# A hybrid layer's second pass reordered: chain slots spread, token rows turned ahead of the second layer's down product

## The reference

```python
x = x + linear_attention(layernorm(x))   # 16 heads, elu(.)+1 feature map, one k^T v matrix per batch, normaliser per head
x = x + ffn(layernorm(x))                # square(relu(x Ws1)) Ws2; routed experts count only where a probability truncates to 1
x = x + small_attention(layernorm(x))    # only the first 16 tokens of each batch, up to 3 softmax iterations; elsewhere a bias row ob
x = x + ffn(layernorm(x))                # the same weights again
```

## Time and profile before

| what | value |
|---|---|
| median of 3 runs (439.25, 441.06, 438.79) | 439.25 us |
| the profiled execution: its time | 441.03 us |
| its span, first to last instruction | 439.2 us |
| PE busy | 404.7 us (92%) |
| DVE busy | 313.5 us (71%) |
| POOL busy | 217.2 us (49%) |
| ACT busy | 204.5 us (47%) |
| mean granted TensorE clock | 0.986 of full speed |

### The profile page before, as it was taken

The page is one execution under the profiler, slowest core; times in us unless marked ns, Lnnn a source line. Parts: engine busy times, 40 slices in busy tenths (PEclk is TensorE's granted clock), DMA queues, the critical chain, the costliest instruction groups (busy, mean ns, idle before and its releaser), DMA issues.

```text
span 439.2 us, 7483 instructions
## 1 busy us (share of the span) xinstructions
PE 404.7 (92%) x2458; PEld 322.7 (73%) x2458; DVE 313.5 (71%) x654; ACT 204.5 (47%) x354; POOL 217.2 (49%) x315
## 2 busy tenths in 40 slices
PE   8898999999999998989989989999899999969983
PEld 5787889988988896777866767677666676747752
DVE  6779976576668666474667688797768877977644
ACT  3766686778778775033324422222342144223340
POOL 3675775776677664032144514662441744533630
PEclk9999999999999999899999999999999999989998
DMA  8701211111100000400011101101110110110022
GB/s 269 236 16 35 80 65 48 49 48 48 48 0 0 1 1 1 99 3 0 6 54 51 52 5 50 52 1 50 49 51 0 51 53 1 50 49 29 22 91 64
DMA packets 22982, 20.64 MB, mean 47 GB/s; under 512 B 3398, under 2 KB 22924, under 8 KB 22924
## 3 DMA queue, kind: packets, MB, share of 16 engines
q1 hardware_dynamic: 22364, 19.40, 14.1%
q10 hardware_dynamic: 560, 0.52, 0.4%
HBM read 11.33 MB, written 8.45 MB: 45 GB/s over the span
## 4 chain that ended last, share of the span: by engine, by line
PE 57%; DVE 18%; ACT 8%; issue 8%; POOL 7%; DVEq 1%; POOLq 0%; ACTq 0%
PE PB L1522 12%; PE PA L1539 11%; PE PT L1557 6%; PE PT L1586 4%; PE PB L1407 3%; ACT scratch L567 3%; PE PG L1358 3%; POOL ln_rstd L444 2%; DVE x_all L1059 2%; ACT scratch L614 2%; POOL ln_rstd L442 2%; DVE ln_bn L797 2%; DVE scratch L1095 2%; ACT xn_pair L578 2%; PE PT L1398 2%
## 5 line engine op out<-in xcount | busy, mean ns | idle before, releaser
L494 POOL TENSOR_TENSOR ln_a<-ln_bn 128x4 f32<-128x4 f32 x32 | 6.7, 210 | 124.2 <-DVE ln_bn L1038 124.2
L1522 PE MATMUL PB<-ws,scratch 128*128 128x256 f32 x248 | 62.3, 395 | 1.9 <-issue 1.9
L1522 PEld LDWEIGHTS PB<-ws,scratch 128*128 128x128 f32 x248 | 46.1, 195 | 20.1 <-issue 14.8
L1539 PE MATMUL PA<-kvwo,q_all 128*128 128x256 f32 x256 | 57.9, 379 | 0.0
L751 ACT ACTIVATE scratch<-PT 128x512 f32<-128x512 f32 x16 | 9.6, 598 | 102.2 <-PE PT L1557 102.2
L1539 PEld LDWEIGHTS PA<-kvwo,q_all 128*128 128x128 f32 x256 | 48.5, 190 | 6.5
L466 POOL TENSOR_TENSOR xn_pair<-scratch,xn_pair 128x1024 fp32r<-128x1024 f32 x16 | 38.5, 2406 | 20.3 <-ACT xn_pair L578 20.3
L882 DVE SCALAR_TENSOR_TENSOR scratch<-scratch,PB 128x512 f32<-128x512 f32 x32 | 20.9, 684 | 38.6 <-ACT scratch L614 38.6
L1038 DVE BATCH_NORM_STATS2 ln_bn<-x_all 128x6 f32<-128x256 f32 x128 | 44.1, 406 | 0.1
L567 ACT ACTIVATE scratch<-x_all,ln_shift,ln_rstd 128x255 f32 (+1 forms) x60 | 31.1, 593 | 22.6 <-POOL ln_shift L448 22.5
L455 POOL TENSOR_TENSOR x_all<-x_all,wvo 128x1024 f32 (+1 forms) x16 | 38.6, 2410 | 0.1
(11 more groups left out here) (252 smaller groups left out, 943.0 us busy)
## 6 DMA issues: line engine op xcount, KB each, us to landing
x_all<-n_L_attn_a_inputs_q_dram SPq DMA_DIRECT2D x15, 512.0 KB, 3.6
out_dram<-x_all SPq DMA_DIRECT2D x15, 512.0 KB, 3.2
out_dram<-x_all SPq DMA_DIRECT2D x2, 256.0 KB, 2.2
x_all<-n_L_attn_a_inputs_q_dram SPq DMA_DIRECT2D x2, 128.0 KB, 3.0
x_all<-n_L_attn_a_inputs_q_dram ACTq DMA_DIRECT2D x2, 128.0 KB, 3.4
setup<-in_L_attn_a_Wk_dram SPq DMA_DIRECT2D x1, 256.0 KB, 4.9
setup<-in_L_attn_a_Wq_dram ACTq DMA_DIRECT2D x1, 256.0 KB, 5.1
wvo<-in_L_attn_a_Wv_dram SPq DMA_DIRECT2D x1, 256.0 KB, 6.4
```

The source lines that it names most:

```text
L1522: last = mm(four(pair)[:, t, :], h[:, t * P:(t + 1) * P], ws2[:, :], start=True, stop=True)
L1539: last = mm(four(PA)[:, t, :], q_all[:, n * C + c, t * P:(t + 1) * P], kvwo[:, b * C + c, :], start=(c == 0), stop=(c == C - 1))
```

## The change

What it does, by engine:

- PE: in a step, R2 stands ahead of F1 (it was behind F4), T2 ahead of F4 (it was behind R2), chain slot 1 ahead of R2, chain slot 2 from step 2 on behind F4, chain slot 3 behind F2. In the last group of the first pass, NP of group 0 stands ahead of the k product (it was behind it).
- DVE: the two inversions are two instructions; that for r opens the step, that for v follows `q_scale`. Chain slot 1 stands ahead of the statistics, h2s ahead of `scaled_sum`, chain slot 3 behind `n_split`. `n_take` and `n_split` of group 0 stand ahead of the last group's k work.
- ACT: it makes the rounded copy n_hi (`n_high`), which DVE made; `scale_tiles` stands behind the copies of T2, chain slot 1 ahead of the relu.
- POOL: the add of the scaled half (now L542) is done a step later, at the step's start, and waits for NP; SP stores a group a step later.

```diff
 # SP
+                u, nu, _ = lagged(g, b, 3)
+                if runs(u):
+                    sp.wait_ge(out_dve, 2 * (u + 1))
+                    sp.wait_ge(out_pool, u + 1)
+                    sp.dma_start(out_dram[bass.ds(nu, 1)].rearrange("o p t d -> p (o t) d"), x_group(nu)).then_inc(stored, 16)
                 if v == NG - 1:
...
-                elif runs(v):
...
-            sp.wait_ge(stored, 16 * (NG - 1))
+            sp.wait_ge(stored, 16 * (NG - 2))
...
 # POOL step
+                if runs(r):
+                    pool.wait_ge(n_mm, min(i + 2, NG))
+                if runs(u):
+                    pool.wait_ge(f4_scaled, 2 * (u + 1))
+                    last = x_all[:, nu * T + 2:(nu + 1) * T, :]
+                    nc.gpsimd.tensor_tensor(last, last, y3, ALU.add).then_inc(out_pool, 1)
                 if runs(r):
...
                     add_row(nr, ob_rows, ob_added)
-                ge(pool, rsq, i - 1)
                 if runs(v):
+                    ge(pool, rsq3, v)
                     four_variances(1, v, bn3, var3)
                 chain(i, 1)
...
-                if runs(v) and v < NG - 1:
-                    pool.wait_ge(f4_scaled, 2 * (v + 1))
-                    last = x_all[:, nv * T + 2:(nv + 1) * T, :]
-                    nc.gpsimd.tensor_tensor(last, last, y3, ALU.add).then_inc(out_pool, 1)
...
 # ACT
+            def n_high(j):
+
+                act.wait_ge(n_inv, j + 1)
+                ge(act, n_op_done, j)
+                nc.scalar.activation(n_hi[:, :], n_sb[:, :], ACT.Copy).then_inc(n_hi_done, 1)
...
                 if i == 0:
+                    n_high(1)
                     fold_ffn()
+                chain(i, 1)
                 if runs(r):
...
-                if runs(v) and v < NG - 1:
-                    scale_tiles(i, v)
-                chain(i, 1)
                 if runs(i):
...
+                if runs(v) and v < NG - 1:
+                    scale_tiles(i, v)
...
                 chain(i, 2)
+                if runs(i + 2):
+                    n_high(i + 2)
...
 # DVE
-                dve.wait_ge(n_inv, 2 * j + 1)
-                nc.vector.tensor_copy(n_hi[:, :], n_sb[:, :]).then_inc(n_inv, 1)
...
+            def reciprocal_variances(slot, j, ready, used, done):
+
+                dve.wait_ge(ready, 5 * (j + 1))
+                ge(dve, used, j if slot == 0 else 2 * j)
+                nc.vector.reciprocal(ln_rsq[:, slot, :], ln_a[:, slot, :]).then_inc(done, 1)
...
+                if runs(r):
+                    reciprocal_variances(0, r, var2, r2_mm, rsq)
                 if runs(i):
...
-                if i > 0:
-                    reciprocal_variances(i, r, v)
+                if runs(v):
+                    reciprocal_variances(1, v, var3, f4_scaled, rsq3)
+                chain(i, 1)
                 if runs(i):
...
-                if runs(v):
-                    scaled_sum(i, v, nv)
-                chain(i, 1)
                 if runs(r):
...
                     nc.vector.tensor_tensor(h2s, h2, PT[:, 1, :], ALU.mult).then_inc(f1_scaled, 1)
+                if runs(v):
+                    scaled_sum(i, v, nv)
                 chain(i, 2)
                 if runs(i + 2):
                     n_take(i + 2)
-                chain(i, 3)
...
                 if runs(i + 2):
                     n_split(i + 2)
+                chain(i, 3)
...
 # PE, first pass
                 ge(pe, k_done, 2 * n)
+                if isinstance(n, int) and n == NG - 1:
+                    n_product(0, 0, 0)
...
                     k_product(n, g, b)
-                    if last and g == G - 1:
-                        n_product(0, 0, 0)
 # PE, step
+                chain(i, 1)
+                if runs(r):
+                    pe.wait_ge(rsq, r + 1)
...
+                    for t in range(T):
+                        last = nc.tensor.transpose(PT[:, 1, t * P:(t + 1) * P], ln_rsq[:, 0, t:t + 1].to_broadcast([P, P]), ident[:, :])
+                    last.then_inc(r2_mm, 1)
                 if runs(r):
...
                     last.then_inc(f1_mm, 1)
+                if runs(i):
+                    pe.wait_ge(w_added, i + 1)
+                    for c in range(C):
+                        for t in range(T):
+                            last = nc.tensor.transpose(PA[:, c, t * P:(t + 1) * P], x_all[:, n * T + t, c * P:(c + 1) * P], ident[:, :])
+                        last.then_inc(t2_mm, 1)
                 if runs(v):
...
                     down(PB if v < NG - 1 else PA, h3, f4_mm)
-                chain(i, 1)
...
+                if i > 1:
+                    chain(i, 2)
...
                     down(PB, h2s, f2_mm)
+                chain(i, 3)
```

More of the change, by code:

```diff
@@ L256, in hybrid_kernel @@
         kvwo_mm, kvwo_done, sel_ready = [sem(n) for n in ("kvwo_mm", "kvwo_done", "sel_ready")]
-        n_mm, n_taken, n_inv, n_op_done = [sem(n) for n in ("n_mm", "n_taken", "n_inv", "n_op_done")]
+        n_mm, n_taken, n_inv, n_hi_done, n_op_done = [sem(n) for n in ("n_mm", "n_taken", "n_inv", "n_hi_done", "n_op_done")]
         bc_mm, q_scaled, w_mm, w_added = [sem(n) for n in ("bc_mm", "q_scaled", "w_mm", "w_added")]
@@ L609, in pass1 @@
                     x_high(n, g)
+                    if last and g == G - 1:
+                        n_high(0)
                     ge(act, q_done, n)
@@ L876, in pass1 @@
                         copy_g(b - 1)
+                    if last and g == G - 1:
+                        dve.wait_ge(sel_ready, 2 + T + 1)
+                        n_take(0)
+                        n_split(0)
                     ge(dve, g_mm, n)
@@ L905, in pass1 @@
                         for t in range(T):
[L906 removed]
+                            nc.vector.memset(low_row[t * 2 * H:t * 2 * H + H, :], 0.0).then_inc(sel_ready, 1)
                         by_half = ident[:, :].rearrange("p (t u k o) -> p t u k o", t=T, u=2, o=1)
                         nc.vector.tensor_tensor(sel[:, :, :].rearrange("p k f -> p (k f)").rearrange("p (t k e) -> p t k e", t=T, e=HD),
[L909 to L910 removed]
+                                                by_half[:, :, 1, :, :].to_broadcast([P, T, H, HD]),
+                                                by_half[:, :, 0, :, :].to_broadcast([P, T, H, HD]), ALU.subtract).then_inc(sel_ready, 1)
                     if last and g == G - 1:
@@ L941, in n_take @@
                 nc.vector.reciprocal(n_sb[:, :], n_sb[:, :]).then_inc(n_inv, 1)
-                dve.wait_ge(n_inv, 2 * j + 1)
-                nc.vector.tensor_copy(n_hi[:, :], n_sb[:, :]).then_inc(n_inv, 1)
             def n_split(j):
-                dve.wait_ge(n_inv, 2 * j + 2)
+                dve.wait_ge(n_hi_done, j + 1)
                 ge(dve, bc_mm, j)
-                nc.vector.scalar_tensor_tensor(n_op[:, :], n_hi[:, :].bitcast(F32), minus_low[:, 0:1], n_sb[:, :],
-                                               ALU.mult, ALU.add).then_inc(n_op_done, 1)
+                nc.vector.scalar_tensor_tensor(n_op[:, :], n_sb[:, :], low_row[:, 0:1], n_hi[:, :].bitcast(F32),
+                                               ALU.mult, ALU.subtract).then_inc(n_op_done, 1)
             def q_scale(j, n, pair):
@@ L1054, in scaled_sum @@
                 dve.wait_ge(f4_mm, v + 1)
[L1055 removed]
+                dve.wait_ge(rsq3, v + 1)
                 if v < B:
@@ L1564, in step @@
                     down(PB if v < NG - 1 else PA, h3, f4_mm)
-                chain(i, 1)
-                if runs(r):
-                    pe.wait_ge(rsq, i)
-                    pe.wait_ge(n_taken, min(i + 2, NG))
-                    ge(pe, f1_scaled, r)
-                    for t in range(T):
-                        last = nc.tensor.transpose(PT[:, 1, t * P:(t + 1) * P], ln_rsq[:, 0, t:t + 1].to_broadcast([P, P]), ident[:, :])
-                    last.then_inc(r2_mm, 1)
-                if runs(i):
-                    pe.wait_ge(w_added, i + 1)
-                    for c in range(C):
-                        for t in range(T):
-                            last = nc.tensor.transpose(PA[:, c, t * P:(t + 1) * P], x_all[:, n * T + t, c * P:(c + 1) * P], ident[:, :])
-                        last.then_inc(t2_mm, 1)
+                if i > 1:
+                    chain(i, 2)
                 if i == 0:
@@ L1582, in step @@
                     pe.wait_ge(kvwo_done, B)
-                chain(i, 2)
+                if i <= 1:
+                    chain(i, 2)
                 if runs(r):
```

26 lines of the change are left out of this document (7 added, 19 removed).

## The result

The changed kernel takes **416.94 us** (median; 414.47 to 418.62), the kernel before 439.04 beside it (438.79 to 441.06): ratio 0.948, 95% interval 0.943 to 0.954, some 22 us or 5% faster. Its profiled execution took 416.83 with a span of 415.0, against 441.03 and 439.2; the difference, 24.2, is the one that the sum of the prediction was made for.

What follows compares the result with a forecast made beforehand. PE sets the pace, busy 152.43 of 162.41 us in steps 2 to 12. Terms -4.2 + 1.0 - 10.3 - 4.7 + 0 + 1.5 = -16.7 give 424.3 profiled, 422.5 as median; range 416 to 427, for all cases 416 to 431.

Steps and rivals of the forecast that it cites:

- End of the first pass, -4.2: End of first pass: NP ahead of the k product removes BC's wait and the half clock, -4.2 us (-2.6 to -4.3).
- Steps 0 and 1, +1.0: Steps 0 and 1: n_high ahead of ACT's copies, and F3 waiting in step 1, +1.0 us (0 to +2).
- Steps 2 to 12, -10.3: Steps 2 to 12: PE's idle and hidden waits, together 11.4, mostly go, -10.3 us (-11.4 to -5).
- Some waits come back: Within steps 2 to 12: waits return, 0.6 us in step 2 and 0.5 after the softmax ending step 10.
- my 12.66: Plain step, start to start: 12.66 us in place of 13.09, with T2 at 0.86, if nothing waits.
- Step 13, -4.7: Step 13: idle and lost clock, 5.9 in all, go; 0.5 and 0.7 return, -4.7 us (-5.9 to -1).
- Steps 14 and 15, 0: Steps 14 and 15: no wait for h2s worth naming, so 0.
- Tail, +1.5: From step 16: F3 later by 0.5 and last stores by 1.0, +1.5 us (-1.2 to +2.5).
- the half clock I leave as it is: Tail: the half clock from 426.7 to 430.1 us stays; were it gone, the time would be 1.7 lower.
- A: Rival: chain slot 1 on DVE, ahead of statistics and h2s, makes F3 wait again; 429 us, chance 0.24.
- B: Rival: R2 and T2 wait for DVE's queue head in some 14 steps, 24 us slower, 446; chance 0.06.
- C: Rival: no change; idle time moves from F3 to R2 and T2, DVE's chain work bounding; 439 us, chance 0.04.

Runs made afterwards that it cites:

- experiment 6: Changed kernel with the end of the first pass put back (NP of group 0 behind the last k product, n_take, copy, n_split on DVE): 418.80 us, ratio 0.951.
- experiment 7: Changed kernel with DVE's bias row instruction of the first pass moved two groups later, behind q_all of group 3: 415.74 us, ratio 0.945.
- experiment 8: Changed kernel with the bias row two groups later and the end of the first pass put back besides: 420.82 us, ratio 0.956.
- experiment 9: Changed kernel with five small moves (bias row, group 1's copy on DVE, step 1's fold products, step 16's order, group 14's store): 409.90 us, ratio 0.932.
- Experiment 3: Changed kernel with T2 put back behind F4 on PE and scale_tiles ahead of T2's copies on ACT: 416.81 us, ratio 0.947.
- experiment 4: Changed kernel with the second pass's rounded copy n_hi back on DVE behind n_take's inversion: 422.30 us, ratio 0.958.
- experiment 1: Changed kernel with one pair of DVE instructions put back, scaled_sum ahead of h2s: 438.36 us, ratio 0.996.
- experiment 2: Kernel before with only one pair of DVE instructions swapped, h2s ahead of scaled_sum: 428.51 us, ratio 0.972.
- experiment 5: Changed kernel with POOL's add of the scaled half put back behind the variances of its own step: 416.87 us, ratio 0.947.

## Why the prediction was right, and where its sum was short

The sign, the likeliest case and the mechanism were right; the forecast of 422.5 is 5.6 high, and the median, 416.94, stands just inside the range of 416 to 427. That it is inside owes something to luck. The lower end, 416, is every term at its lower bound, taken from the median before; taken from the profiled execution, for which the sum was made, the same bounds end at 418.2, and 416.83 lies 1.4 below. (The upper end, 427, is not the sum of the upper bounds, which makes 435.) On that scale the sum said -16.7, and -24.2 came; the 7.5 are 3.5 in steps 2 to 12, 1.4 in step 13, 0.7 in steps 14 and 15, and 1.9 in the tail. By its terms, on the profiled executions:

1. *End of the first pass, -4.2:* 4.13, and no half clock from BC to W. Right, and shown by experiments 6 to 8.
2. *Steps 0 and 1, +1.0:* +0.92, in the two places named (copy ahead of the fold copies, 0.43 by experiment 9; F3's wait in step 1, 1.20).
3. *Steps 2 to 12, -10.3:* 13.84. **This term was mis-sized**, by 3.5, and 2.4 beyond its own lower bound. "Some waits come back" failed: the 0.6 of step 2 and the 0.5 of step 11 did not come (12.59 and 14.01 long, no idle time). And the plain step went to 12.43, below my 12.66, since I took only F3's wait as hidden and left F1, F4 and F3 at the lengths of the earlier trace rows. They were longer than their work: F1 to the next piece 1.82, now 1.72; F4 1.80, now 1.73; F3 1.06, now 0.95. In the earlier trace rows F4 starts 0.11 behind the end of `q_scale`, for which it waits (232.55 and 232.44): a wait too short to be shown under the modelled end of F1. Experiment 3, where F4 again follows F1 directly but starts 0.47 behind the end of `q_scale`, keeps 1.72 and 1.72 in step 3:

```profile
225.67 1.88 PE L1575 MATMUL PT<-scratch,ffn_weights 128*128 128x512 f32 x4
225.71 1.21 DVE L969 TENSOR_TENSOR q_all<-q_all,PB 128x1024 f32<-128x1024 f32 x1
227.39 1.89 PE L1532 MATMUL PB<-ws,scratch 128*128 128x256 f32 x8
229.11 1.04 PE L1587 MATMUL PA<-ident,x_all 128*128 128x128 f32 x8
```

In its steps 11 and 13 F4 starts 0.10 behind that end, and there both take 1.80 again.
4. *Step 13, -4.7:* 6.11. The mechanism was right: L1242's successor, away from POOL, takes 0.35, and the clock stays whole. The 1.2 that were to come back were mostly not there; F3 waits 0.19:

```profile
364.99 0.35 DVE L1252 TENSOR_SCALAR b_weights<-b_weights,q_all 128x256 f32<-128x256 f32 x1
```

```profile
367.43 1.12 PE L1599 MATMUL PT<-scratch,ffn_weights 128*128 128x512 f32 x2 [0.19 <-DVE scratch L1103]
```

5. *Steps 14 and 15, 0:* step 14 is 0.15 shorter, step 15 0.51.
6. *Tail, +1.5:* 0.4 shorter from step 16 on. The waits came where they were forecast (R2 2.63 behind the stretch's start, forecast 2.8; F1 3.1, forecast 3.2; h2s ready 7.1, forecast 7.2), and the last stores land in 3.3 instead of 2.2. **What failed is "the half clock I leave as it is".** F1 of step 16, first in the changed kernel, then in the kernel with the bias row later:

```profile
397.83 0.65 PE L1567 MATMUL PT<-ident,ln_rsq 128*128 128x128 f32 x4 [0.99 <-DVE ln_rsq L1057]
398.32 1.88 PE L1575 MATMUL PT<-scratch,ffn_weights 128*128 128x512 f32 x4
```

```profile
396.75 0.66 PE L1571 MATMUL PT<-ident,ln_rsq 128*128 128x128 f32 x4 [0.98 <-DVE ln_rsq L1061]
397.23 3.58 PE L1579 MATMUL PT<-scratch,ffn_weights 128*128 128x512 f32 x4
```

The same pieces behind the same waits (0.71 and 0.99 or 0.98): at the full clock here, at 0.50, the 1.2 GHz level, there. With the fall the term would have been +1.3, close to the forecast. Nor need it take another kernel: of the changed kernel's nine executions six have a mean granted clock of 0.994 to 0.996 and three of 0.989 to 0.991, these 1.2 to 1.8 us longer than the profiled one beside them; that fits one such fall, but both profiles are of the first kind, so it is not seen. One trace of the kernel before could not have told it, and what decides it stays open. The rule of the Trainium skill on transposes, which the prediction weighed (TensorE: Matmul & The Clock Gate, Part 4), does not separate the two either, as the transposes are the same in both.

The rivals: A (the chain's waits come back) shows only as the 0.19 of step 13. B named the right place, DVE's queue head, as experiment 4 shows: with DVE held for one add, R2 and BC are late. Its price, 24, was too high by far: 5.5 came from W of step 0 to W of step 15, the tail's clock left out. C did not come: the whole is 22 us faster, not the same.

What the prediction did not have is how the gain divides. From W of step 0 to W of step 15 the kernel before takes 225.18, with the one pair swapped 213.63, changed 206.00: 11.6 for h2s ahead of `scaled_sum`, then 7.6 for everything else. That division holds in this order only: with the pair put back (experiment 1) the stretch takes 224.73, so everything else is worth 0.45 without the pair, and the pair 18.7 with everything else in place. The 7.6 lie mostly in steps with chain work, 4.3 in steps 6 to 8 and 2.8 in steps 11 to 13, and 0.3 to 0.4 in each of steps 2 to 5; steps 0 and 1 lose 0.9. No run puts R2 or the chain's slots back by themselves, so which of them brings it is not shown.

## What to carry to other kernels

When a product waits for an engine, look first at what stands ahead of the awaited instruction in that engine's own queue, and whether it waits for something later: here one swapped pair brought half of 22 us by itself, without it the rest of the change brought some 2, and it also removed a stretched instruction two places away. A product can wait though no idle time is shown: here F1 and F4 together took 3.62 where F4 started 0.1 behind the end of what it waits for, and 3.44 where it started 0.47 behind. So count a product's whole distance to the next start against an undisturbed one. Before two kernels are compared by their medians, compare the stretches that the edit cannot touch: here 2 us at a place 130 us away hid half of an effect of 4.

## What the runs showed of the hardware

DVE and POOL can hold each other until the other's instruction ends. With starts 0.04 to 0.05 apart a 128x256 DVE operation took 0.48 or 2.72, POOL's add 2.71 or 2.40, and the first pass 2 us less or more; the starts, DVE's ahead in both, do not tell which one is held. A 128x128 copy took 2.40 beside a 2.35 add, 0.23 alone.

Waits of 1.56 in each step (experiment 1) left the mean granted clock of steps 2 to 14 at 1.00. The wait of 2.57 or 2.58 at the end of the first pass was followed by half clock in each of the four kernels that had it (before, and experiments 2, 6 and 8); the waits of 0.71 and 0.99 in the tail were so in three kernels (experiments 4, 7 and 8), and not in six profiles with the same waits (the changed kernel twice, and experiments 1, 3, 5 and 6).
